# Operands of VectorE's products moved from SBUF into PSUM, beside a queue of indirect gathers

## The reference, cut to what matters

```python
def spline_conv(x, row, col, basis, idx, W, b):
    z = jnp.einsum('ni,kio->nko', x, W).reshape(N * K, Fout)      # K = 125
    gathered = z[col[:, None] * K + idx]
    msg = jnp.einsum('es,eso->eo', basis, gathered)
    out = jax.ops.segment_sum(msg, row, num_segments=N)
    return out / jnp.maximum(deg, 1.0)[:, None] + b
...
h = jnp.ones((N, 1), x.dtype)
h = jax.nn.elu(spline_conv(h, row, col, basis, idx, stn1_w, stn1_b))
h = jax.nn.elu(spline_conv(h, row, col, basis, idx, stn2_w, stn2_b))      # 64 -> 64: c2
h = jax.nn.elu(h @ stn3_w + stn3_b)
t = h @ stn4_w + stn4_b
new_pseudo = jnp.clip(pseudo + t[col] - t[row], 0.0, 1.0)
return spline_conv(x, row, col, basis2, idx2, conv_w, conv_b)             # 32 -> 32: c3
...
e = jax.nn.leaky_relu(el[src] + er[dst], 0.2)
ee = jnp.exp(e - emax[dst])
alpha = ee / denom[dst]
msg = feat[src] * alpha[:, :, None]
agg = jax.ops.segment_sum(msg, dst, num_segments=N)
```

## Time and profile before

| | before |
|---|---|
| runs | 10834.07, 10852.45, 10830.36 us, median 10834.07 |
| profiled execution | 10832.76 us, span 10831.0 us, mean granted clock 0.778 |
| busy over the span | PE 54%, PEld 46%, DVE 71%, ACT 27%, POOL 64% |
| DMA | 608.41 MB, mean 56 GB/s |
| c2 | first gather at 3477.73 us of the span, last copy out of `mix` at 5972.69 |
| c3 | from there to 8258 us |
| attention | from some 8420 us to the end |

### The profile page before, as it was taken

How to read it: one execution, slowest core, us unless ns; L and a number is a source line. 1 busy time by engine, 2 the same in 40 slices (tenths; PEclk the granted TensorE clock), 3 DMA queues, 4 the chain that set the end, 5 groups by cost and what they waited for, 6 DMA issues and landing times. The chain is left out here.

```text
span 10831.0 us, 178896 instructions
## 1 busy us (share of the span) xinstructions
PE 5813.8 (54%) x38968; PEld 4935.1 (46%) x38968; DVE 7688.3 (71%) x17252; ACT 2905.0 (27%) x8407; POOL 6940.1 (64%) x6574
## 2 busy tenths in 40 slices
PE   3366666665574799999999355555555000000000
PEld 2255555555474577777777355555554000000000
DVE  9966666665697577777777476776774388888888
ACT  0022222222232344443444244444442011111111
POOL 6077777777001777777774677777770677777773
PEclk9977877887797899999999688888886555555555
DMA  1030000001933454555554344444442222222221
GB/s 47 6 111 3 3 3 3 3 3 4 29 41 53 94 99 100 101 100 99 100 100 87 51 68 68 68 68 68 68 68 33 46 58 59 53 59 58 59 58 45
DMA packets 2181778, 608.41 MB, mean 56 GB/s; under 512 B 2007975, under 2 KB 2141607, under 8 KB 2181476
## 3 DMA queue, kind: packets, MB, share of 16 engines
q1 hardware_dynamic: 1078132, 311.05, 15.0%
q0 software_dynamic: 218016, 193.97, 9.3%
q10 hardware_dynamic: 885584, 102.89, 7.4%
HBM read 430.75 MB, written 176.23 MB: 56 GB/s over the span
## 5 line engine op out<-in xcount | busy, mean ns | idle before, releaser
L1228 PE MATMUL c_acc<-c_spread_sb,c_basis_sb 128*125 128x256 f32 (+1 forms) x12544 | 2461.6, 363 | 1159.6 <-DVE c_basis_sb L1103 865.6
L1228 PEld LDWEIGHTS c_acc<-c_spread_sb,c_basis_sb 128*125 128x125 f32 x12544 | 2166.5, 221 | 1422.5 <-issue 1045.8
L1651 POOL DMA_INDIRECT at_ring<-gat_table,at_place x1568 | 1652.8, 1054 | 757.4 <-issue 757.1
L976 POOL DMA_INDIRECT c_ring<-hid_table,c_at x1568 | 1715.7, 1094 | 639.5 <-issue 442.0
L614 POOL DMA_INDIRECT rec<-rk_rec,rk_place x1568 | 1645.4, 1049 | 517.3 <-issue 469.3
L976 POOL DMA_INDIRECT c_ring<-feat_table,c_at x1568 | 1622.8, 1035 | 518.9 <-issue 440.2
L1353 ACT ACTIVATE c_sums<-c_acc 125x512 f32<-125x512 f32 (+1 forms) x3136 | 1448.1, 492 | 1877.8 <-PE c_acc L1228 1486.1
L1087 DVE TENSOR_TENSOR c_spread_sb<-c_mark,c_rin 128x512 f32<-128x512 f32 (+1 forms) x3136 | 1745.2, 557 | 60.2
L1908 PE MATMUL gr_hps<-ident,gr_hs 128*32 128x128 f32 x98 | 29.8, 408 | 2146.7 <-DVE gr_xs L1742 2146.7
L1908 PEld LDWEIGHTS gr_hps<-ident,gr_hs 128*32 128x32 f32 x98 | 6.3, 108 | 2161.1 <-DVE gr_xs L1742 2161.1
L1240 PE MATMUL c_mix<-c_sums,c_w 125*64 125x256 f32 (+1 forms) x9408 | 906.0, 390 | 102.9 <-ACT c_sums L1353 102.9
(11 more groups left out here) (362 smaller groups left out, 9179.2 us busy)
## 6 DMA issues: line engine op xcount, KB each, us to landing
c_rin<-rows SPq DMA_DIRECT2D x3136, 42.0 KB
c_rin<-rows SPq DMA_DIRECT2D x3136, 20.0 KB
rows<-c_ring ACTq DMA_DIRECT2D x408, 128.0 KB, 2.4
rows<-c_ring ACTq DMA_DIRECT2D x408, 72.0 KB
rows<-rk_blank SPq DMA_DIRECT2D x112, 252.0 KB
rows<-at_ring SPq DMA_DIRECT2D x196, 144.0 KB
rec<-rk_rec,rk_place POOLq DMA_INDIRECT x1568
c_ring<-hid_table,c_at POOLq DMA_INDIRECT x1568
```

The costliest lines, as they stand in the source:

```text
L976: pool.indirect_dma_start(out=ring[:, u, j, :], out_offset=None, in_=table, in_offset=bass.IndirectOffsetOnAxis(ap=at[:, h, u, j:j + 1], a ...
L1228: last = pe.matmul(acc[pp % BANKS][:, (w % 2) * WN * feats:(w % 2 + 1) * WN * feats], basis[:, q, w, :, :].rearrange("p a b -> p (a b)"), ...
L1651: pool.indirect_dma_start(out=ring[:, u, j, :], out_offset=None, in_=d.gat_table, in_offset=bass.IndirectOffsetOnAxis(ap=place[:, u, j:j + ...
```

## The change

In `flow_conv` the tiles `mark` and `plane` leave SBUF and share one PSUM bank, `mesh`; `mark` has one buffer where it had two. The banks `mix` and `back` become two parts of one bank. TensorE's identity matmul, which writes into `back`, now waits until ScalarE has copied `mix` out. In `attention_flow` the tile `weight` moves from SBUF to PSUM. No other instruction is added or removed.

```diff
@@ flow_conv
-        mark = sb(f"{name}_mark", [P, 2, GW2, WN])
-        plane = sb(f"{name}_plane", [P, GW2, 5, 5])
...
-        mix = ps(f"{name}_mix", [P, 512])
-        back = ps(f"{name}_back", [P, 512])
+        mix_bank, mesh = ps(f"{name}_mix", [P, 512]), ps(f"{name}_mesh", [P, 512])
+        mix, back = mix_bank[:, 0:2 * P], mix_bank[:, 2 * P:2 * P + 2 * outs]
+        mark = mesh[:, 0:GW2 * WN].rearrange("p (g r) -> p g r", r=WN)
+        plane = mesh[:, GW2 * WN:GW2 * (WN + 25)].rearrange("p (w a b) -> p w a b", a=5, b=5)
...
-                        dve.tensor_tensor(spread[:, q, w, :, :], bc(mark[:, q, w, :].unsqueeze(2), [P, 2, feats, WN]),
+                        dve.tensor_tensor(spread[:, q, w, :, :], bc(mark[:, w, :].unsqueeze(2), [P, 2, feats, WN]),
...
                 pe.wait_ge(added, item + 1)
+                pe.wait_ge(mixed_taken, item + 1)
                 pe.matmul(back[:, 0:2 * outs], c.ident[:, :],
                           conv_out[:, bass.ds(i * 2, 2), :].rearrange("p b o -> p (b o)"), start=True, stop=False,
                           skip_group_check=True)
-                pe.wait_ge(mixed_taken, item + 1)
@@ attention_flow
-        weight = sb("at_weight", [P, 2, RUN + 1, HEADS])
+        weight = ps("at_weight", [P, 2, RUN + 1, HEADS])
```

More of the change, by code:

```diff
@@ L1092, in make_mark @@
                 def make_mark():
-                    dve.tensor_tensor(mark[:, q, :, :], bc(rel[:, :].unsqueeze(2), [P, GW2, WN]),
+                    dve.tensor_tensor(mark[:, :, :], bc(rel[:, :].unsqueeze(2), [P, GW2, WN]),
                                       c.ramp[:, q * GW2 * WN:(q + 1) * GW2 * WN].rearrange("p (g r) -> p g r", r=WN),
@@ L1131, in body @@
                 dve.tensor_tensor(tsel[:, :, :, :].rearrange("p g r k -> p (g r) k"),
-                                  bc(mark[:, q, :, :].rearrange("p g r -> p (g r)").unsqueeze(2), [P, GW2 * WN, 3]),
+                                  bc(mark[:, :, :].rearrange("p g r -> p (g r)").unsqueeze(2), [P, GW2 * WN, 3]),
                                   trow[:, q, :, 0:3], ALU.mult).then_inc(seq, 1)
```

## The result

| | before | after |
|---|---|---|
| median of the runs | 10843.26 us (10830.36 to 10857.5) | 10567.7 us (10560.46 to 10569.67) |
| ratio | | 0.9745, 95% interval 0.9732 to 0.9757 |
| profiled execution | 10832.76 us | 10569.67 us, span 10567.9, mean granted clock 0.782 |

What follows compares the result with a forecast made beforehand. POOL was taken to bound the attention, POOL's holds to delay TensorE in c2, and SP to bound c3. From 10832.8 us, 158 (attention) and 94 (c2) came off: 10,580 us forecast, range 10,530 to 10,710.

Steps and rivals of the forecast that it cites:

- What bounds it: Attention paced by POOL issuing gathers; in c2 POOL's holds reach TensorE through ScalarE's stores; c3 paced by SP's load issue.
- Marks, planes and weights in PSUM: Product, spreads and basis get one PSUM input, ending POOL's hold; it stays for small operations with both inputs in SBUF.
- Rival C: POOL's hold stays, since the other input and output remain in SBUF; about 10,853 us; chance 0.04.
- Attention: Attention stage: a pair of blocks falls from 46.24 to 42.8 us, 158 us gained over 46 pairs; POOL still ends last.
- the holds that stay: Attention: 0.45 us a pair added for holds beside small operations with both inputs in SBUF, a chosen share of 3.9.
- c2: First large convolution: a pair falls from 48.79 to 46.7 us as gathers come early enough; 94 us gained over 45 pairs.
- The identity matmul: TensorE, behind ScalarE's copy out of the mixing bank: stands bare once a pair, costing 0.4 us, on the path in c2.
- c3: Second large convolution: no gain, since SP's issue is untouched; 44.4 us a pair stays.
- Price of a PSUM operand: VectorE's instructions with a PSUM operand: between 0 and 55 ns more each; taken as 0.
- rival A: VectorE: each PSUM operand costs 55 ns, so c3 pays 64 us; 10,645 us; chance 0.12.
- D: VectorE reads the repeated PSUM patterns at half rate, slowing attention, c2 and c3; about 12,700 us; chance 0.08.
- Rival B: c2 does not gain, as ScalarE's store waits for something else; only the bare identity matmul remains; 10,692 us; chance 0.10.

## Why the prediction was right

**What bounds it.** Attention by POOL: shown, by the gathers that shrank and the pair that shrank with them. c2 by late gathers, through ScalarE's stores, to TensorE: shown by TensorE's wait, which went, and by the mark and plane runs, in which only the place of one input changes and the time rises once the gathers are late enough.

**Marks, planes and weights in PSUM.** That the hold ends with one PSUM input was read from a scatter beside L492 in the sort; it holds for all three kinds of product. That the hold stays for the small steps was right too (L1098 above). Rival C (the hold stays) is out. The Trainium skill, SBUF — State Buffer, section "Who interferes with whom", has it as a rule: a VectorE instruction with two SBUF inputs contends with a GpSimd one that reads SBUF, one with at most one SBUF input, outside VectorE's 2-port modes, does not. The traces agree, 1054 and 946 ns.

**Attention.** The term was 158 us, measured 171. The mis-sized part is the share for "the holds that stay", 0.45 us a pair, which I chose: 42.52 measured against the 42.2 counted from below and 42.8 forecast. The short steps with two SBUF inputs do hold, but few gathers meet them: the 40 that start under the first score step (L1781) take 987 ns in the mean and up to 1.11 us, and with a mean of 946 ns over all gathers against 944 of an undisturbed one this comes to 0.06 us a pair. VectorE is next, as said, but at 41.39 and not 41.65, since L1797 and the exponential got shorter.

**c2.** 46.74 us a pair against 46.7, 92 us against 94. By the waits: 1.59 - 0.05 = 1.5 us a pair of waiting gone, 1.7 us of half-speed clock gone from 20 of the 49 pairs, 0.7 on average, and 0.4 paid for the identity; that makes 1.8 of the 2.05 us. That 92 meets 94 so closely is in part luck: by the medians the convolutions' share is 109 us, and the same c2 code took 2342 us in the profile of before and 2356 in that of the attention alone. The 46.14 that the forecast starts from is also the last pair but one; the last is 46.24.

**The identity matmul.** 0.4 us was right (46.56 against 46.16 in the median, with and without it), but not as a cost against before: alone on the kernel before it costs nothing that can be measured. It is a price that the changed kernel pays because the gathers no longer cover it. Rival C's 20 us had the same flaw.

**c3.** Nothing, as forecast, 44.41 us a pair on both sides. But "SP never stops, so nobody else's time counts there unless it grows" was sharper than I knew: 0.5 us more on ScalarE a quarter cost 1.9 us a pair at once, so the slack was far under the 0.9 us that I read from VectorE's wait for the move table. Had rival A been true, it would probably have cost c3 more than I gave it; no run shows that.

**Price of a PSUM operand.** 0, as taken: L1811 1489 ns on both sides. Rivals A (55 ns) and D (half rate) are out. The Trainium skill, VectorE: DVE Perf Modes, section on the TRN2 errata, would have 62 cycles more for a source in PSUM. These traces don't show it: L1087 takes 690 ns where it took 692. Rival B is out, since c2 gained.

## What to carry to other kernels

When an engine's own instructions grow beside another engine's, list what the other ran at that moment and where its inputs lay; here it was one input in SBUF too many, and one bank of PSUM a phase freed POOL. Price an added wait in the profile that the change will leave, not in the one it starts from: the same 0.4 us was free behind a late gather and cost 24 us once the gather was early. An engine that never idles may have a loop just under it; take work off both at once, or the first edit looks like a loss.

## What the runs showed of the hardware

- One PSUM input is enough to end the hold on POOL's indirect gathers. The gather beside a product with two SBUF inputs took 1.22 to 2.23 us, beside one with a PSUM input 0.94. An output in PSUM is not enough: beside L1098, with two SBUF inputs, a gather of 1.31 us remains.
- VectorE's strided reduction (L1797, 160 elements read four apart) takes 325 ns from PSUM and 432 from SBUF; ScalarE's exponential of 164 elements in place 292 and 339 ns.
- A wait of 1.59 us on average ahead of c2's mixing went with some 1.7 us more of the mixing itself in 24 of 49 pairs (each with 2.9 to 4.4 us at granted clock 0.50); with the wait gone 4 of 49 are left.
